# Two-block gated cross-attention and FFN kernel on one core: homes of the normalised x tiles, place of the prior logarithm, and order of the last program

## The reference, cut to what matters

```
x = x + tanh(g_xattn[0]) * attention0(layernorm(x), ctx)    # 32 query heads, 8 kv heads of 128, rope
x = x + tanh(g_ffn[0])   * quantised_ffn(layernorm(x))      # 512 -> 1376 -> 512, 4-bit weights, 8-bit activations
x = x + tanh(g_xattn[1]) * channel_attention(layernorm(x), ctx)   # 512 x 512 scores per batch, 64 channels
x = x + tanh(g_ffn[1])   * lora_ffn(layernorm(x))

def lora_ffn(x):                       # x: 16 x 64 x 512
    y = x @ W_base.T + b_base
    contribs = ((x @ A[active]) @ B[active]) * 2          # 4 active experts of 16, rank 8
    logits = (x @ router_W.T + router_b)[active]
    alpha = softmax(log(domain_prior[active] + 1e-12) + logits)
    return y + sum(contribs * alpha)
```

## Time and profile before

| what | value |
|---|---|
| median of three runs | 806.31 us (804.34 to 806.90) |
| profiled execution | 806.67 us, span 804.9 us from first to last instruction |
| granted TensorE clock, mean | 0.999 |
| PE busy | 789.9 us, 98% of the span |
| DVE, ACT, POOL busy | 587.6, 445.2, 503.5 us |

### The profile page before, as it was taken

The page is one execution under the profiler, slowest core; times in us unless marked ns, Lnnn a source line. Parts: engine busy times, 40 slices in busy tenths (PEclk is TensorE's granted clock), DMA queues, the critical chain, the costliest instruction groups (busy, mean ns, idle before and its releaser), DMA issues.

```text
span 804.9 us, 13826 instructions
## 1 busy us (share of the span) xinstructions
PE 789.9 (98%) x5062; PEld 645.6 (80%) x5062; DVE 587.6 (73%) x1092; ACT 445.2 (55%) x843; POOL 503.5 (63%) x429
## 2 busy tenths in 40 slices
PE   8999999999999999999999999999998999999997
PEld 7888888888888888888888888888755777778786
DVE  5867988768888655786656565555999988888763
ACT  4754455454445434444444433433579998887772
POOL 1597567745756764565677455556357788777662
PEclk9999999999999999999999999999999999999999
DMA  9411331422333231734112211277236223331101
GB/s 303 132 67 31 113 94 40 125 75 58 93 89 90 63 101 46 37 91 113 63 40 69 64 28 27 39 92 285 58 92 150 67 59 99 100 79 47 47 15 40
DMA packets 72259, 66.76 MB, mean 83 GB/s; under 512 B 35921, under 2 KB 51505, under 8 KB 71809
## 3 DMA queue, kind: packets, MB, share of 16 engines
q1 hardware_dynamic: 71520, 65.56, 31.6%
q10 hardware_dynamic: 672, 0.33, 0.1%
HBM read 49.04 MB, written 6.34 MB: 69 GB/s over the span
## 4 chain that ended last, share of the span: by engine, by line
PE 90%; DVE 3%; POOL 2%; ACT 2%; DMA 1%; issue 1%; SPq 1%; ACTq 0%; DVEq 0%; POOLq 0%
PE bank L87 12%; PE bank L88 11%; PE bank L89 11%; PE bank L530 7%; PE bank L525 7%; PE bank L526 7%; PE bank L507 7%; PE bank L653 4%; PE bank L1656 4%; PE bank L1642 3%; PE bank L1608 2%; PE bank L640 2%; PE bank L1632 2%; PE bank L1587 2%; PE bank L1633 2%; PE bank L1579 1%
## 5 line engine op out<-in xcount | busy, mean ns | idle before, releaser
L963 DVE SCALAR_TENSOR_TENSOR x_res<-bank,gate,x_res 128x512 f32<-128x512 f32 x128 | 94.2, 745 | 67.0 <-PE bank L530 66.7
L1244 POOL TENSOR_TENSOR prob<-prob,row_inv 128x512 f32<-128x512 f32 x32 | 33.5, 1048 | 161.5 <-DVE row_inv L959 161.5
L1230 POOL TENSOR_TENSOR rope_swap<-rope_swap,trig 128x512 f32<-128x512 f32 x80 | 106.0, 1325 | 35.9 <-ACT rope_swap L722 35.6
L721 ACT COPY rope_swap<-bank 64x512 f32<-64x512 f32 x80 | 46.8, 585 | 107.8 <-DVE rope_cos L934 107.7
L87 PE MATMUL bank<-xnT_hi,wq_hi 128*128 128x512 f32 x256 | 103.0, 403 | 0.0
L525 PE MATMUL bank<-wo_hi,oT_hi 128*128 128x512 f32 x256 | 101.7, 397 | 0.7 <-issue 0.5
L88 PE MATMUL bank<-xnT_lo,wq_hi 128*128 128x512 f32 x256 | 101.4, 396 | 0.0
L89 PE MATMUL bank<-xnT_hi,wq_lo 128*128 128x512 f32 x256 | 101.1, 395 | 0.0
L526 PE MATMUL bank<-wo_lo,oT_hi 128*128 128x512 f32 x256 | 100.9, 394 | 0.0
L934 DVE TENSOR_TENSOR rope_cos<-bank,trig 128x512 f32<-128x512 f32 x80 | 54.6, 683 | 61.6 <-PE bank L89 61.5
L1236 POOL TENSOR_TENSOR q_rope<-rope_cos,rope_swap 128x512 f32<-128x512 f32 x64 | 84.4, 1319 | 5.0
(11 more groups left out here) (255 smaller groups left out, 2021.7 us busy)
## 6 DMA issues: line engine op xcount, KB each, us to landing
wq_raw<-in_L_xattn_wq SPq DMA_DIRECT2D x16, 512.0 KB, 4.1
wo_raw<-in_L_xattn_wo SPq DMA_DIRECT2D x16, 512.0 KB, 3.8
xn<-in_L_ffn_Wd SPq DMA_DIRECT2D x16, 256.0 KB, 3.4
b_ctx<-in_ctx SPq DMA_DIRECT2D x32, 128.0 KB, 2.7
b_k_twice<-b_qk_hi SPq DMA_DIRECT2D x32, 128.0 KB, 2.4
w_T_dram<-w_out SPq DMA_DIRECT2D x28, 128.0 KB, 2.8
w_T<-w_T_dram SPq DMA_DIRECT2D x2, 1376.0 KB, 18.6
xn<-in_L_ffn_Wg SPq DMA_DIRECT2D x10, 256.0 KB, 3.8
```

Of the source, the lines that this page charges most:

```text
L963: dve.scalar_tensor_tensor(out=K.x[:, t, :], in0=wo_ps[t % 2][:, :], scalar=K.gate[:, 0:1], in1=K.x[:, t, :], op0=ALU.mult, op1=ALU.add).t ...
L1230: pool.tensor_tensor(out=sw, in0=sw, in1=sin_b, op=ALU.mult).then_inc(s_rope, 1)
```

## The change

**Opening.** `x_home` lists five homes for normalised tiles: the three `xn` buffers, `prob[1]` and `prob[0]`. Tile t goes to `x_home[t % 5]`, so only tiles 5, 6, 7 take over a used one. ACT normalises tiles 0, 1, 2, 3 and 5; DVE tiles 4, 6, 7. `shift_tiles` computes `x_shift` with one small `tensor_scalar` per tile, each with its own count on the semaphore.

**Prior.** ACT takes the logarithm of the 16 raw priors in slot 30, after `first_split_hi(1)`, and calls a Tanh on a scratch column right behind. In slot 31 DVE adds it to the raw router bias and spreads the sum (`router_offset`); `low_T` has one matmul for it instead of two and ACT copies the result straight into `logit_row`. `ln_prior`, `rest_of_weights` and `bias_prior` are gone.

**Last program.** The same calls stand in another order on PE, DVE, ACT, POOL and SP. The body is untouched otherwise.

```diff
-        XN_ACT = (0, 1, 2, 4, 5)
-        XN_DVE = (3, 6, 7)
+        XN_ACT = (0, 1, 2, 3, 5)
+        XN_DVE = (4, 6, 7)
+        x_home = xn + [prob[k][:, :, :, :].rearrange("p t b k -> p (t b k)") for k in (1, 0)]
+        NHOME = len(x_home)
...
-                for i in range(2):
-                    mm = pe.matmul(trans[:, HD + i * E_ACT:HD + (i + 1) * E_ACT], M.spread[i][:, :], M.sel_e[:, :], start=True, stop=True)
-                mm.then_inc(s_w_lowT, 1)
+                pe.matmul(trans[:, HD:HD + E_ACT], M.spread[:, :], M.sel_e[:, :], start=True, stop=True).then_inc(s_w_lowT, 1)
...
             def normalise_tile(t):
                 act.wait_ge(s_rstd, t // UT + 1)
-                act.wait_ge(s_x_shift, t // UT + 1)
-                if t >= 3:
-                    act.wait_ge(s_tr, NT + t - 2)
+                act.wait_ge(s_x_shift, t + 1)
+                if t >= NHOME:
+                    act.wait_ge(s_tr, NT + t - NHOME + 1)
...
-            for t in range(3):
+            for t in range(UT):
                 normalise_tile(t)
...
-            def ln_prior():
-                act.wait_ge(M.s_w_low, 1)
-                act.activation(M.log_prior[:, :], M.bias_prior[:, E_ACT:2 * E_ACT], ACT.Ln, bias=K.log_eps[:, :]
-                               ).then_inc(M.s_w_ln, 1)
+            def prior_logarithm():
+                act.wait_ge(R1.s_in, 16 * R1.n_loads)
+                act.activation(R1.prior[:, :], R1.prior[:, :], ACT.Ln, bias=K.log_eps[0:E_ALL, :]).then_inc(M.s_w_ln, 1)
+                act.activation(M.lsum[0:E_ALL, :], K.log_eps[0:E_ALL, :], ACT.Tanh)
...
                         first_split_hi(0)
                         first_split_hi(1)
+                        prior_logarithm()
...
-                part = slice(half * UT, (half + 1) * UT)
                 dve.wait_ge(s_rstd, half + 1)
-                dve.scalar_tensor_tensor(out=x_shift[:, part], in0=meanvar[:, part, 0], scalar=-1.0, in1=rstd[:, part],
-                                         op0=ALU.mult, op1=ALU.mult).then_inc(s_x_shift, 1)
+                for t in range(half * UT, (half + 1) * UT):
+                    dve.tensor_scalar(x_shift[:, t:t + 1], meanvar[:, t, 0:1], rstd[:, t:t + 1], -1.0, ALU.mult, ALU.mult
+                                      ).then_inc(s_x_shift, 1)
...
-            normalise_tile(3)
+            normalise_tile(UT)
...
+            def router_offset():
+                dve.wait_ge(M.s_w_ln, 1)
+                dve.tensor_tensor(out=R1.rb[:, :], in0=R1.rb[:, :], in1=R1.prior[:, :], op=ALU.add).then_inc(s_sel, 1)
+                dve.wait_ge(s_sel, 10)
+                dve.tensor_copy(M.spread[:, :], R1.rb[:, :].to_broadcast([E_ALL, P])).then_inc(s_sel, 1)
...
                     base_low_part(1)
                     gated_rows()
+                    router_offset()
```

More of the change, by code:

```diff
@@ L752, in _ @@
                 hi_tile(n)
[L753 to L754 removed]
+            normalise_tile(UT + 1)
             evacuate(0, 5)
@@ L1802, in tensor @@
+            down(1)
+            weights_T(1, 4)
+            pe.wait_ge(s_qk_lo[0], 4)
+            x_transpose(3)
+            x3_T(0)
+            logits(2, 1)
+            weights_T(1, 5)
+            pe.wait_ge(s_up, 9)
+            up_mm(3, 0)
+            low(0)
+            pe.wait_ge(s_out, 2)
             gate_mm(3, 0)
-            weights_T(1, 1)
-            pe.wait_ge(s_up, 9)
-            h_transpose_b(1)
+            weights_T(1, 6)
+            logits(2, 2)
+            logits(2, 3)
@@ new lines, in tensor @@
+            pe.wait_ge(s_gate, 23)
+            h_transpose_a(6)
+            lora(3)
+            pe.wait_ge(s_up, 23)
+            h_transpose_b(6)
+            logits(6, 6)
+            weights_T(6, 2)
+            x3_T(4)
+            pe.wait_ge(s_hTa_sb, 7)
+            gate_mm(7, 2)
+            logits(6, 7)
+            pe.wait_ge(s_hTb_sb, 7)
+            up_mm(7, 2)
+            weights_T(6, 3)
+            low(4)
+            logits(7, 0)
+            weights_T(6, 4)
+            pe.wait_ge(s_gate, 24)
@@ new lines, in tensor @@
+            down(6)
+            z_T(4)
+            weights_T(6, 5)
+            logits(7, 1)
+            logits(7, 2)
+            weights_T(6, 6)
+            base(4)
+            weights_T(6, 7)
+            lora(4)
+            logits(7, 3)
+            pe.wait_ge(s_qk_lo[1], 8)
+            v_item(6)
+            x3_T(5)
+            logits(7, 4)
+            weights_T(7, 0)
+            low(5)
+            attend_pair(6, 0)
+            attend_pair(6, 1)
+            pe.wait_ge(s_up, 24)
@@ L2342, in vector @@
+            make_h(1, 2)
+            lo_qk(3, 1)
+            scale_up(2, 0)
+            h_scales(1)
+            reciprocal(1, 1)
+            scale_gate(2, 1)
+            row_max(1, 4)
             scale_up(2, 1)
-            row_max(1, 3)
-            h_scales(1)
+            front(3)
+            row_max(1, 5)
+            first.low_b_lo()
+            row_max(1, 6)
             make_h(2, 0)
-            row_max(1, 4)
+            reciprocal(1, 2)
+            residual(0)
             scale_gate(2, 2)
-            reciprocal(1, 1)
+            row_max(1, 7)
@@ L2409, in vector @@
+            make_h(3, 2)
+            h_scales(3)
+            lo_qk(5, 0)
             reciprocal(3, 0)
             row_max(3, 2)
+            residual(2)
+            row_max(3, 3)
+            row_max(3, 4)
+            scale_gate(4, 0)
+            reciprocal(3, 1)
+            route(1)
+            front(5)
+            row_max(3, 5)
+            route_end(1)
+            output(3)
+            scale_up(4, 0)
+            row_max(3, 6)
+            reciprocal(3, 2)
+            row_max(3, 7)
@@ L2540, in vector @@
+            output(6)
+            zT_lo(4)
+            row_max(7, 1)
+            row_max(7, 2)
+            statistics(6)
+            make_h(7, 1)
+            shift_of(6)
+            make_h(7, 2)
             reciprocal(7, 0)
-            row_max(7, 2)
             finish(4)
-            statistics(7)
+            h_scales(7)
+            route(5)
             row_max(7, 3)
             row_max(7, 4)
-            shift_of(7)
-            route(5)
-            route_end(5)
-            reciprocal(7, 1)
@@ L2558, in vector @@
+            statistics(7)
+            reciprocal(7, 3)
+            shift_of(7)
             finish(5)
```

1467 lines of the change are left out of this document (689 added, 778 removed).

## The result

The changed kernel took 800.99 us (median of four runs, 799.35 to 801.46) against 806.36 us for the kernel before on the same chip (four runs, 804.34 to 806.90): 5.4 us less by the medians. The ratio of the two kernels is put at 0.9939 (95% interval 0.9925 to 0.9953), which is 4.9 us less. The forecast was 803.4 us, 2.9 us less, with an 80% range of 800.5 to 806.2. The direction was right and the time lies in that range, near its lower end. The profiled execution took 801.0 us, with a span of 799.0 us.

What follows compares the result with a forecast made beforehand. PE's own work was taken to bound the kernel, so only its gaps could move. Terms -1.2 - 0.2 + 0.1 - 1.5 + 0.4 - 0.5 = -2.9 us gave 803.4 us, 80% range 800.5 to 806.2.

Steps and rivals of the forecast that it cites:

- The opening: Up to 60 us: PE's wait for normalised tile 3 on DVE goes whole, -1.2 us (0 to -1.4).
- The matmul: `low_T`: PE has one matmul less, -0.2 us.
- The logarithm in slot 30: Slot 30: 3.1 us of ACT work fit in its 3.94 us idle behind the context splits, cost 0.
- The sum of bias and prior: Slot 31: two small DVE instructions ahead of `oT_lo` overfill 0.28 us of idle time, +0.1 us (0 to +0.4).
- The start: Last program, 588 to 628.5 us: new order brings the first `down` earlier, -1.5 us (-0.3 to -4.3).
- up to 1.3 by itself: Last program: taking away the uncovered second table load, ahead of PE's waits, is worth up to 1.3 us.
- The middle: 628.5 to 780 us: small waits likely at `v_item` soon after `down`, +0.4 us (0 to +2.0).
- The end: Last tile: `v_item(7)` covers the second `weights_T` wait and `lora(6)` goes into a gap, -0.5 us (0 to -0.9).
- The waits only move: Rival, chance 0.22: busy DVE limits the start's gain to -0.3 us and the end wins nothing; 805.1 us.
- The start closes: Rival, chance 0.16: PE finds work at each wait, -4.3 us at the start, middle loses nothing; 800.2 us.
- The switch that overruns slot 30: Rival, chance 0.04: each table switch holds ACT 1.4 us longer, PE waits about 1.9 us for `probT`; 805.3 us.
- The starved middle: Rival, chance 0.07: `down` to `v_item` takes 7.0 us, six short tiles cost 1.1 us each; 809.6 us.

Runs made afterwards that it cites:

- logarithm back: Changed kernel with the prior's logarithm back in the last program and two matmuls in `low_T`; ratio 0.9952, 803.7 us.
- opening alone: Kernel before with only the new opening (five homes, tile 3 on ACT, one small shift per tile); ratio 0.9992, 806.2 us.
- pairs apart: Changed kernel with a call put between the two back-to-back `attend_pair` calls of tiles 1, 2, 3, 5 and 6; ratio 1.0036, 810.2 us.
- changed again: Changed kernel rerun without edits on a second chip; ratio 0.9928, 802.3 us.
- pairs together: Changed kernel with the second attention pair of tiles 0 and 4 moved right behind the first; ratio 0.9965, 804.9 us.
- logarithm twice: Changed kernel with a second logarithm and tanh on scratch columns in slot 30, two table switches more; ratio 0.9969, 804.8 us.
- shifts of four: Changed kernel with four columns of `x_shift` in one instruction again, as before; ratio 0.9946, 801.9 us.
- the first four experiments: Kernel before with only the new opening (0.9992) or prior (0.9995); changed kernel with the old opening (0.9947) or logarithm back in the last program (0.9952).
- later scales: SP's weight-scale stores one step later: changed kernel 808.7 us, kernel before 812.2 us, changed kernel also with `router_offset` ahead of `statistics_end` 807.9 us.

## Why the prediction was right, and where not

**The premise failed in part.** "The change hardly alters PE's work, so it can only move these gaps" is the step that was wrong. One matmul is as good as nothing of the work, but the order is not. PE's own time from slot 31 to the last attention was 211.0 to 211.1 us in the three traces of the table with the old lists. It is 208.8 to 209.7 in the four with the new ones. At equal work (logarithm back against opening alone) the difference is 1.4 us. The sum had no term for it, and that is most of the 2 us by which it fell short. Two places where it went can be read. Five tiles have their attention pairs back to back, 5 x 0.15 = 0.75 us. And the first product of a `logits` has a price that goes with what stands ahead of it. Two places in the changed kernel, behind a run of bf16 products and behind another `logits`:

```profile
773.18 0.58 PE L1636 MATMUL bank<-b_k_twice,b_q_stack 128*128 128x512 f32 x1
773.61 0.39 PE L1637 MATMUL bank<-b_k_lo,b_q_stack 128*128 128x512 f32 x1
...
755.87 0.40 PE L1637 MATMUL bank<-b_k_lo,b_q_stack 128*128 128x512 f32 x1
756.10 0.40 PE L1636 MATMUL bank<-b_k_twice,b_q_stack 128*128 128x512 f32 x1
756.34 0.39 PE L1637 MATMUL bank<-b_k_lo,b_q_stack 128*128 128x512 f32 x1
```

From its start to the next it takes 0.43 us in the first and 0.24 in the second; behind a group of transposes it is 0.32. In the kernel before 15 of the 64 stand behind gate or up products and 14 behind other float32 products of 512 columns; after it, 10 and 19. All 64 together went from 20.7 to 19.7 us. Part of both is given back elsewhere (`qk` 0.5 us more, the transposes of h 0.5 more). The traces show that the order is worth this; that the weight loads hidden behind a neighbour are the reason is not shown.

**The opening**, -1.2: it was 1.44 us in the stages, in three traces against four. From the transposes of tiles 0 to 2 to that of tile 3 it took 2.70 us (24.75 to 27.45) and takes 1.31 (24.65 to 25.96). That is 1.39 us for a wait shown as 1.24: it cost 0.15 us more than its length. What was to be late next was not: PE has no wait for `xnT_lo`. The term was 0.2 us short.

**The matmul**, -0.2: as said. **The logarithm in slot 30**, 0: as said, with 0.84 us to spare; with two switches more PE waits 1.8 us, so the cover that I named is the right one.

**The sum of bias and prior**, +0.1 (0 to +0.4): 0 in the profile after, 0.7 us in six traces of nine, outside my bounds. I priced the copy by a row of slot 30, where POOL was idle. I had looked at who waits for `oT_lo`, and not at what POOL does at that moment. The Trainium skill (page "SBUF — State Buffer", section "Who interferes with whom") says that a DVE copy in a two-port mode and a POOL instruction take one port pair in turns, each for the whole instruction. The traces agree: 1.97 us beside the memsets, 0.21 away from them. No row names the copy's mode; that it was a two-port one is inferred.

**The start**, -1.5 (-0.3 to -4.3): against the profile of before, idle time there fell by 2.9 us, and the first `down` starts at 609.32 instead of 613.01, 2.6 us more than the lead of the opening. That looks like a term mis-sized by half, and it is mostly the base. The profile of before was a long one in this stretch: the kernel with the opening alone, with the same lists, idles 3.17 us from slot 31 to the first `down` instead of 4.30, because the 0.7 us behind the copied keys and the 0.3 us behind `f_up` are absent. I had kept the wait for the copied keys as fixed. From 3.17 to the 1.57 us of the changed kernel it is 1.6 us, the size that I gave.

The two edits seem to be worth more together than apart. The logarithm's move takes 1.1 us off the last stage in the old order, near my "up to 1.3 by itself", and 1.9 to 2.0 in the new, each without the wait for `oT_lo`. In the old order DVE's work stood right behind (0.8 and 0.4 us of it appear at once). This rests on one trace on either side of each difference; the times of the runs are too wide to show it.

**The middle**, +0.4 (0 to +2.0): the one wait that opened is 0.27 us, behind a `v_item` for `b_xn`, the chain that I named:

```profile
761.39 1.13 PE L1623 MATMUL bank<-l_v,b_xn 128*128 128x128 f32 x8 [0.27 <-ACT b_xn L2624]
```

The other 0.54 us of idle time in the stretch to 780 is the wait of `weights_T(7, 5)` (see the end). The six short tiles did not starve PE: from `down` to `v_item` they take 8.3 to 8.8 us, of which 5.9 to 6.4 are other work, and five of the six have no wait. From the first `down` to the last attention it is now 2.2 us less (177.22 to 174.99): there PE's own time outweighs what waits opened.

**The end**, -0.5: the row of `weights_T(7, 4)` to `attend_pair(7, 0)`:

```profile
777.07 0.60 PE L1646 MATMUL bank<-ident,b_e 128*128 128x128 f32 x4
...
778.43 0.63 PE L1646 MATMUL bank<-ident,b_e 128*128 128x128 f32 x4 [0.54 <-ACT b_eT L2650]
...
782.15 1.97 PE L1660 MATMUL bank<-b_eT,b_v 128*64 128x128 f32 x32
```

The second row is `weights_T(7, 5)` with the wait that it had before. In all it is 5.08 us against 4.71 in the earlier trace rows, with 0.9 us of `v_item(7)` in it: -0.53, and one wait instead of two, as I had it. The tail is the same.

**All together.** From the kernel with the opening alone to the changed one the last stage is 3.85 us shorter, 1.80 of idle time and 2.05 of PE's own. With 1.44 us of the opening that is 5.3 us, and the medians are 5.4 us apart.

**The rivals.** "The waits only move" (805.1 us) is out for the whole change, since 1.57 us of idle time are left up to the first `down`; of the prior's move alone in the old lists it is nearly true. "The start closes" (800.2 us) gave the nearer number, and not by its mechanism: 1.6 us stay idle at the start, and 1.4 us or more came from PE's own time. That the measured time fell inside my 80% range is in part luck, since the range was stretched down for this rival and not for what happened. The switch that overruns slot 30 is out by direct test. The starved middle did not come, though one tile of the six had begun to wait. The kernel with pairs apart shows how near another form of it was: a few moved calls made it 0.4% slower than the kernel before, by waits for other copies than the one that I named.

## What to carry to other kernels

Where one engine is busy nearly all the time, its order is also a price and not only a set of waits: read what the same instruction costs behind each kind of neighbour before saying that an order can only move gaps. Read a small instruction's price beside what the other engine on its port does at that moment, and judge a wait from more than one trace, since some of those summed here were in one execution and not in the next. Take the idle time to be won from more than one trace too: here one execution had 1.1 us of waits that its twin with the same lists did not have. Two edits that each remove one of two waits standing in a row may be worth more together than the sum of both, which these traces suggest and do not prove.

## What the runs showed of the hardware that was not expected

The wait in the middle of the body. In six traces (changed, changed again, pairs together, logarithm twice, shifts of four, pairs apart) PE waited 0.6, 1.3, 1.8, 2.4, 2.6 and 3.5 us for an `x_res` of DVE near 340 us, and in the first four experiments not at all. DVE, which has nothing to wait for there but PE's product, is idle before it, for 3.64 to 4.65 us in the three longest, which the profile puts down to "remote". What holds it is open; the kernels with later scales only tie it to the store of the scales or to what stands beside it.

What such a wait costs is more than its length. TensorE in the kernel with pairs apart, by stretches, columns as in the earlier trace rows:

```profile
336.00:340.00 4.00, 3.09 (x14) 2.16 (x12) 0.75 (x1) 2.59 (x5) 3.79 (x4) 1.00 1.73 26
340.00:344.00 4.00, 1.46 (x4) 1.17 (x5) 2.23 (x4) 0.00 (x0) 2.01 (x2) 0.71 0.51 14
344.00:348.00 4.00, 4.00 (x18) 3.60 (x16) 0.96 (x2) 0.59 (x1) 0.00 (x0) 0.50 0.41 22
348.00:352.00 4.00, 4.00 (x29) 3.66 (x28) 2.07 (x3) 0.32 (x1) 0.00 (x0) 0.50 0.50 127
352.00:356.00 4.00, 4.00 (x13) 3.19 (x12) 2.08 (x4) 2.25 (x5) 1.01 (x1) 0.59 0.00 0
356.00:360.00 4.00, 4.00 (x19) 3.23 (x18) 2.61 (x5) 1.78 (x3) 1.43 (x3) 1.00 0.12 27
```

PE has no work for 3.5 us, until 342.54. The granted clock falls within that wait to 0.50, the 1.2 GHz level, and stays there to about 355 us, some 13 us with PE busy throughout. It is back at 1.00 in the last row. The body of that trace is 522.5 us, 9.7 over the usual 512.8: 3.5 of wait and about 6 of clock. The wait of 2.6 us (shifts of four) gave 520.4, with a clock of 0.50 from 344 to 352 us. One of 1.3 us (changed, again) left the clock at 1.00 and the body at 514.5. It shows in the times too: of the 29 executions of the kernel before on the third chip, the 24 up to 807.8 us have a mean clock of 0.999 or 1.00 but for one, and the five from 808.3 us on all have 0.998. So the long executions go with a fallen clock. The spread of some 3 us among the others is not explained by it, and both are the reason that the times of single parts say less here than the stages.
